# Experts in two groups of tiles, the back stage and most of the combine inside the tile loops

## What is computed

```
h  = layernorm(x) * gamma + beta;  u, z = split(h @ in_proj)      # 256 channels each
uc = silu(conv4(u) + b);  dt, B, C = split(uc @ x_proj)
delta = softplus(dt @ dt_proj + b)
state[t] = exp(delta * A) * state[t-1] + delta * B * uc           # 256 x 16 states, over 2048 steps
y  = (sum_n state * C + uc * D) * silu(z)
x1 = layernorm(2 * x + y @ out_proj)
scores = softmax(x1 @ Wg + bg);  take the 2 best of 8 experts per token
e(x) = gelu(x @ W1[e] + b1[e]) @ W2[e] + b2[e]                    # 128 -> 512 -> 128
out = layernorm(x1 + p1 * e1(x1) + p2 * e2(x1))
```

## Time and profile before

| what | value |
|---|---|
| runs, median of three | 786.08 us (785.85 to 788.13) |
| the profiled execution, its own time | 791.61 us |
| its span, first to last instruction | 789.9 us |
| mean granted clock of TensorE | 0.913 of full |
| busy share: PE, DVE, ACT, POOL | 75%, 85%, 54%, 71% |
| scans, VectorE L1382 | 256, 312.9 us |
| products with C, GpSimd L553 | 128, 301.0 us |
| tiles, VectorE L1533 | 71 |
| scatters, GpSimd L673 | 71, 69.8 us |
| mean DMA rate | 149 GB/s |

### The profile page before, as it was taken

One profiled execution on the slowest core, in us unless ns is written; L12 is line 12 of the kernel. 1 busy time (PEld: TensorE's weight loads), 2 busy tenths in 40 slices (PEclk: granted clock), 3 DMA queues, 4 the chain that ended last, 5 costly groups with the idle time before them and its releaser, 6 DMA issues. The chain is left out here.

```text
span 789.9 us, 11864 instructions
## 1 busy us (share of the span) xinstructions
PE 592.4 (75%) x3055; PEld 290.2 (37%) x3071; DVE 670.4 (85%) x1349; ACT 428.5 (54%) x886; POOL 562.2 (71%) x538
## 2 busy tenths in 40 slices
PE   9768788887887888788788674676440999998920
PEld 4322222222322222222222121211130899998910
DVE  4287999999999999999998999999823688887855
ACT  3858586577467476657746554334110565555515
POOL 3345877776899799889879788878865356665634
PEclk9899999999999999999999788878755999999975
DMA  3095476566579568647556654864003677776644
GB/s 93 17 224 133 101 172 154 120 160 161 133 163 258 130 160 191 141 119 186 136 132 152 144 124 104 200 158 109 28 28 102 169 201 215 209 211 176 194 167 169
DMA packets 51169, 117.34 MB, mean 149 GB/s; under 512 B 8816, under 2 KB 25008, under 8 KB 43040
## 3 DMA queue, kind: packets, MB, share of 16 engines
q1 hardware_dynamic: 45344, 107.20, 55.7%
q0 software_dynamic: 4320, 8.99, 3.5%
q10 hardware_dynamic: 1440, 0.40, 0.2%
HBM read 100.21 MB, written 16.35 MB: 148 GB/s over the span
## 5 line engine op out<-in xcount | busy, mean ns | idle before, releaser
L553 POOL TENSOR_TENSOR hc<-hs,Crep 128x1024 f32<-128x1024 f32 x128 | 301.0, 2357 | 96.1 <-DVE hs L1382 85.8
L1382 DVE TENSOR_TENSOR_SCAN hs<-bank,state,flow 128x512 f32<-128x512 f32 x256 | 312.9, 1267 | 17.8 <-ACT bank L1125 11.6
L1125 ACT ACTIVATE bank<-bank,negA 128x512 f32<-128x512 f32 x256 | 164.1, 659 | 186.2 <-PE bank L798 182.6
L798 PE MATMUL bank<-delta,sel 64*128 64x512 f32 x512 | 156.7, 691 | 96.6 <-DVE hs L1382 96.2
L1365 DVE TENSOR_TENSOR flow<-flow,bank 128x2048 f32<-128x2048 f32 x63 | 142.9, 2268 | 0.0
L1266 ACT ACTIVATE flow<-bank,b1T 128x128 f32<-128x128 f32 x284 | 80.8, 369 | 57.1 <-PE bank L988 28.7
L798 PEld LDWEIGHTS bank<-delta,sel 64*128 64x128 f32 x512 | 41.8, 198 | 188.7 <-DVE hs L1382 163.6
L673 POOL DMA_INDIRECT results<-flow,idn x71 | 69.8, 983 | 33.1 <-issue 31.3
L807 PE MATMUL bank<-hc,kc 128*32 128x512 f32 x512 | 73.2, 647 | 7.8 <-POOL hc L553 7.8
L996 PE MATMUL bank<-w_sb,flow 128*128 x568 | 75.5, 276 | 4.5 <-ACT flow L1266 3.3
L988 PE MATMUL bank<-flow 128*128 128x128 f32 x568 | 76.8, 279 | 0.0
(11 more groups left out here) (196 smaller groups left out, 793.3 us busy)
## 6 DMA issues: line engine op xcount, KB each, us to landing
flow<-du_d SPq DMA_DIRECT2D x63, 1024.0 KB
flow<-L_ffn_W SPq DMA_DIRECT2D x71, 256.0 KB
xg<-xs SPq DMA_DIRECT2D x71, 66.0 KB
du_d<-du SPq DMA_DIRECT2D x28, 128.0 KB
xin<-L_attn_x SPq DMA_DIRECT2D x8, 256.0 KB, 3.6
hs<-results SPq DMA_DIRECT2D x8, 256.0 KB, 4.7
out<-hc SPq DMA_DIRECT2D x8, 256.0 KB, 2.0
results<-flow,idn POOLq DMA_INDIRECT x71
```

The source lines that it names most:

```text
L553: nc.gpsimd.tensor_tensor(hc[:, Q % 2, two, :], hs[:, Q % 2, two, :], Crep[u % 3][:].unsqueeze(1).broadcast_to([P, 2, T]), ALU.mult).then_ ...
L798: ins = nc.tensor.matmul(dbank[2 * odd + i][:], sel[rows, odd, q % 4, :], delta[u % 2][rows, q // 4, :])
L1125: nc.scalar.activation(dbank[G % 4][:], dbank[G % 4][:], ACT.Exp, scale=negA[:, ch:ch + 1]).then_inc(s_ex, 1)
L1382: nc.vector.tensor_tensor_scan(hs[:, Q % 2, j, :], dbank[G % 4][:], flow[Q % 3][:, j, :], state[:, Q // QUADS % 2, Q % QUADS, j:j + 1], AL ...
```

## The change

The constants first: the units are parted into a group of six and one of two, each with its own tiles and its own half of xs.

```diff
-MAXT = 2 * NTOK // P + E - 1
+GROUP_UNITS = (6, 2)
+GROUP_TILES = [2 * T * n // P + E - 1 for n in GROUP_UNITS]
+GROUP_AT = (0, GROUP_TILES[0])
+FACTS = 4
+MAXT = sum(GROUP_TILES)
+SUMS_AT = 62
+GROUP_ROWS = (E * REGION + E) * P
+PLANNED = (14, 29)
```

That makes 55 and 23 tiles, MAXT = 78. The plan is now a function plan(p, step). Its fifteen steps for group 0 (the fourteen of before, and a copy that sets run to the second group's bases) stand behind the scans of the last host, one behind each of g = 8 to 22:

```diff
+                    if 8 <= g < 23 and j == UNITS - 1:
+                        plan(0, g - 8)
```

The tile loop of group 0 starts when these and the rows of units 0 to 5 are there. The buffers of the loop move from flow to rooms that are free by then (pre, relu, hT, gated), and the banks to ones that the back stage doesn't use, so that one bank is left for the transposed tile:

```diff
-                after(pe, e_xe, n - 1)
-                nc.tensor.transpose(xT_bank[n % 2][:, 0:P], xg[:, n % 8, 0:D], ident[:]).then_inc(e_xT, 1)
+                after(pe, e_xe, n)
+                nc.tensor.transpose(xT_bank[:, 0:P], xg[:, n % 8, 0:D], ident[:]).then_inc(e_xT, 1)
```

The back stages of units 6 and 7 go into the loop's iterations: on TensorE at the end of an iteration, on VectorE behind finish_tile, on ScalarE ahead of the gelu, on GpSimd ahead of the scatter. In this order the four pieces:

```diff
+            def back_of_last(n):
+                if n == 0:
+                    add_states(QUADS * UNITS - 2)
+                if n == 2:
+                    add_states(QUADS * UNITS - 1)
+                if n == 3:
+                    ranks(last - 1)
+                if n == 5:
+                    out_proj(last, (0, 1))
+                if n == 6:
+                    out_proj(last, (2, 3))
+                if n == 14:
+                    xn_T(last)
+                if n == 16:
+                    logits(last)
+                if n == 19:
+                    ranks(last)
...
+            def back_of_last(n):
+                if n == 4:
+                    post(last, 1)
+                if n == 5:
+                    dve.wait_ge(s_plan, PLANNED[0] + 1)
+                    ranks(last - 1)
+                if n == 7:
+                    place(last - 1)
+                if n == 8:
+                    residual(last)
+                if n == 9:
+                    back_stats(last)
+                if n == 17:
+                    best_two(last)
+                if n == 18:
+                    one_hots(last)
+                if n == 20:
+                    ranks(last)
+                if n == 23:
+                    place(last)
+                if 24 <= n < 38:
+                    plan(1, n - 24)
...
+            def back_of_last(n):
+                if n == 13:
+                    xns(last)
+                if n == 15:
+                    xnT_evac(last)
+                if n == 20:
+                    gate_exp(last)
+                if 27 <= n < 27 + E:
+                    fill_tail(n - 27)
...
+            for n in range(MAXT + 3):
+                if n == 5:
+                    mask_ranks(last - 1)
+                if n == 9:
+                    places(last - 1)
+                    tag_rows(last - 1)
+                if 10 <= n < 10 + 4 * TT and n % 2 == 0:
+                    list_rows(last - 1, (n - 10) // 2)
+                if n == 11:
+                    back_rstd(last)
+                if n == 19:
+                    shift_ex(last)
+                if n == 22:
+                    mask_ranks(last)
+                if n == 25:
+                    places(last)
+                    tag_rows(last)
+                if 26 <= n < 26 + 4 * TT and n % 2 == 0:
+                    list_rows(last, (n - 26) // 2)
+                if n >= 3:
+                    scatter(n - 3)
+                if SUMS_AT + 3 <= n < SUMS_AT + 3 + 2 * GROUP_UNITS[0] and (n - SUMS_AT) % 2 == 1:
+                    final_rstd((n - SUMS_AT - 3) // 2)
```

The tags are read for four tiles at once, in five instructions on four columns, behind the copy of every fourth tile:

```diff
+            def row_facts(m):
+                n, last = FACTS * m, min(FACTS * m + FACTS, MAXT)
+                ring, those = slice(n % 8, n % 8 + last - n), slice(n, last)
+                rows = xg[:, ring, :]
+                for k in range(n, last):
+                    dve.wait_ge(e_g[k % 8], 16 * (k // 8 + 1))
+                nc.vector.tensor_tensor(is_second[:, ring], rows[:, :, D + 1], expert[:, those], ALU.not_equal).then_inc(e_k, 1)
+                nc.vector.tensor_tensor(is_first[:, ring], rows[:, :, D + 1], expert[:, those], ALU.is_equal).then_inc(e_k1, 1)
+                dve.wait_ge(e_k, m + 1)
+                nc.vector.tensor_tensor(extra[:, ring], is_second[:, ring], rows[:, :, D + 3], ALU.mult).then_inc(e_ex, 1)
+                for k in range(n, last):
+                    after(dve, e_sc[k % 8], 16 * (k // 8))
+                nc.vector.scalar_tensor_tensor(idn[:, ring], is_second[:, ring], float(NTOK), rows[:, :, D],
+                                               ALU.mult, ALU.add).then_inc(e_id, 1)
+                dve.wait_ge(e_ex, m + 1)
+                nc.vector.tensor_tensor(prob[:, ring], extra[:, ring], rows[:, :, D + 2], ALU.add).then_inc(e_pr, 1)
```

```diff
+                if SUMS_AT + 1 <= n < SUMS_AT + 1 + 2 * GROUP_UNITS[0] and (n - SUMS_AT) % 2 == 1:
+                    add_pair((n - SUMS_AT - 1) // 2)
+                    moments2((n - SUMS_AT - 1) // 2)
```

More of the change, by code:

```diff
@@ L468, in _, with rows_ready @@
                 load_w1(n)
[L469 to L479, removed]
+            def rows_ready(p):
+                sp.wait_ge(s_plan, PLANNED[p])
+                sp.wait_ge(s_fill, 32)
+                sp.wait_ge(s_tail, 16 * E * (p + 1))
+                for b in range(B):
+                    sp.wait_ge(s_scat[b], 128 * sum(GROUP_UNITS[:p + 1]) // 2)
+            rows_ready(0)
             def load_sum(u):
@@ L602, in host @@
                 for slot in range(2 * QUADS):
+                    if slot == 15 and not late:
+                        shift_ex(j - 1)
                     times_c(QUADS * j + slot // 2, slot % 2)
@@ L1011, in _ @@
                     output(n - 2, chosen[n - 2])
+                back_of_last(n)
         @block.scalar
@@ L1268, in gelu, with finals @@
                 ins.then_inc(e_ge, 1)
-            act.wait_ge(s_plan, 14)
-            for n in range(MAXT):
-                gelu(n, index(etab[0:1, n:n + 1], mybir.EngineType.Activation, E - 1))
-            for u in range(UNITS):
+            def finals(u):
                 act.wait_ge(s_fr2, 2 * u + 2)
@@ L1279, in _ @@
                 ins.then_inc(s_fin, 1)
+            act.wait_ge(s_plan, PLANNED[0])
+            act.wait_ge(s_dl, 2 * UNITS)
+            for n in range(MAXT):
+                if n == GROUP_AT[1]:
+                    act.wait_ge(s_plan, PLANNED[1])
+                back_of_last(n)
+                if SUMS_AT + 4 <= n < SUMS_AT + 4 + 2 * GROUP_UNITS[0] and (n - SUMS_AT) % 2 == 0:
+                    finals((n - SUMS_AT - 4) // 2)
+                gelu(n, index(etab[0:1, n:n + 1], mybir.EngineType.Activation, E - 1))
+            for u in range(GROUP_UNITS[0], UNITS):
+                finals(u)
         @block.vector
@@ L1493, in _ @@
                 host(j)
-            last = UNITS - 1
-            ranks(last - 1)
-            place(last - 1)
-            post(last, 1)
-            residual(last)
-            back_stats(last)
-            best_two(last)
-            one_hots(last)
-            ranks(last)
-            place(last)
-            drained(dve, fill_of(last, "ranks"))
-            planned = [0]
-            def plan(ins):
-                planned[0] += 1
-                ins.then_inc(s_plan, 1)
-                dve.wait_ge(s_plan, planned[0])
-            plan(nc.vector.tensor_copy(tail[:], run[:]))
-            plan(nc.vector.tensor_tensor(count[:], run[:], base, ALU.subtract))
-            plan(nc.vector.tensor_tensor(over, count[:].unsqueeze(2).broadcast_to([P, E, ROOM]),
-                                         thresholds.unsqueeze(1).broadcast_to([P, E, ROOM]), ALU.is_gt))
-            plan(nc.vector.reduce_sum(tiles[:], over, AX_X))
-            plan(nc.vector.tensor_tensor_scan(cum[:], one8, tiles[:], 0.0, ALU.mult, ALU.add))
-            cums = cum[:].unsqueeze(1).broadcast_to([P, MAXT, E])
-            plan(nc.vector.tensor_tensor(past, numbers.unsqueeze(2).broadcast_to([P, MAXT, E]), cums, ALU.is_ge))
-            plan(nc.vector.tensor_tensor(pastc, past, cums, ALU.mult))
-            plan(nc.vector.reduce_sum(region[:], past, AX_X))
-            plan(nc.vector.reduce_max(first[:], pastc, AX_X))
-            plan(nc.vector.tensor_tensor(within[:], numbers, first[:], ALU.subtract))
-            plan(nc.vector.scalar_tensor_tensor(lrow[:], region[:], float(REGION), within[:], ALU.mult, ALU.add))
-            plan(nc.vector.tensor_scalar(expert[:], region[:], float(E - 1), None, ALU.min))
-            plan(nc.vector.tensor_copy(rtab[:], lrow[:]))
-            plan(nc.vector.tensor_copy(etab[:], expert[:]))
             def x_evac(n):
```

210 lines of the change are left out of this document (124 added, 86 removed).

## The result

The changed kernel takes 817.1 us (median of four runs, 816.4 to 817.7) where the kernel before takes 786.5 (785.9 to 788.1): a ratio of 1.039, 95% interval [1.037, 1.040]. The forecast was slower, 790.5. The direction is right and the size is not: the kernel takes 26.6 us more than forecast. Its profiled execution has a span of 814.9.

A forecast was written before the change was run, and what follows sets the result against it. It took VectorE to bound the hosts, nothing the idle stretch, and TensorE, with VectorE nearly as tight, the tile loop. Terms, including +13.3 for seven more tiles, sum to +4.4 on the median 786.08: 790.5 us, range 779 to 801.

The forecast's parts named there:

- The step that failed: Tile loop: GpSimd takes in its former idle-stretch work over 36 tiles, the ring of eight lending the rest; +0.5 us, bound 8.
- the one on GpSimd as the loop's bound (801): Slower rival, tile loop: a scatter costs GpSimd 1.90 us, not 1.38, adding 10.5 us; 801 us, chance 0.04.
- Back stage off the path: Before the tile loop: group 1 starts once unit 5's rows are listed, first transposition at 574.5 instead of 611.61; −37.1 us.
- plan in the last host: Fifteen VectorE plan steps between scans: 5.8 us of their own plus 3.5 for waits on GpSimd products; +9.3 us.
- the prediction's sign of being wrong (within 6): End of the scans: the prediction is wrong if the last scan ends within 6 us of 569.9.
- The full exclusion (803.5): Slower rival, last host: every two-input plan step waits for a GpSimd product, 16.5 us instead of 3.5; 803.5 us, chance 0.03.
- Insertions in group 1: Group 1's tile loop: added work costs +9.0 us on TensorE, +5.9 on VectorE, +1.6 on ScalarE, +0.5 on GpSimd.
- Tags: VectorE's tile loop: tags for four tiles at once delay the finish in one iteration of four; +2.1 us, bounds 0 and 6.
- Combine in the loop: Group 2's tiles: six units' combine, each alone between finish and copy every second iteration; +13.0 us, half-clock bound 3.2 more.
- Combine out of the end: Kernel's end: six units' combine at 2.20 us each leave it; −13.2 us.
- the rival in which the change cancels: Last host: the plan steps' 3.5 us of waits on neighbours don't occur; 787.0 us, chance 0.20.
- The faster rival: VectorE's tile loop: the freed tag time is usable, so insertions and tags cost less; 781.1 us, chance 0.25.

The follow-up runs named there:

- three edited forms on chip 4: Kernel after with lists writing 512 bytes per row, tags one tile at a time, or each list behind its iteration's scatter: 790.1, 788.9 and 788.5 us.
- doubled scatter: Kernel before with a second scatter at each of 19 tiles: 789.3 us on chip 14, 831.1 us (1.051) on chip 6.
- unchanged kernel: Kernel after with no further edit, against the kernel before: 817.2 us (chip 13), 818.5 (chip 6), 788.4 (chip 7).
- the last experiment: Kernel after with lists behind scatters and VectorE's inserted steps ahead of the finish, on chip 7: 779.9 us, 0.992 of the kernel before.
- lists last alone: Kernel after with each list issued behind its iteration's scatter instead of ahead, on chip 13: 820.1 us, 1.039 of the kernel before.
- four edits: Kernel after without the sixteen lists, with 512-byte list rows, with tags per single tile, or with lists behind scatters: 793.0, 790.1, 788.9, 788.5 us.
- two of the controls: Kernel before with a plain SP DMA, or a GpSimd product, added at 19 tiles, on chip 14: 787.7 and 817.2 us.

## Why the prediction was off, point by point

**The step that failed** is the one on GpSimd: "+0.5, bound 8". It asked whether GpSimd has the time for sixteen lists beside the scatters. It has: on chip 7, and in three edited forms on chip 4, the lists are in the loop and the kernel takes 788.4 to 790.1, within about 2 us of the forecast. What the step did not ask is what close indirect DMAs do to others. In the first measurement, as on 13 and 6, they hold TensorE's completions back: 117.3, 116.5 and 118.1 us for group 1, where chip 7 needs 95.1 (581.25 to 676.38). So this term is 21 to 23 us, and about 5 more between tiles 41 and 64 (50.3 against 44.9 on chip 7), 4 of them in the three tiles at the run of close scatters from tile 49 on. No rival had it: the one on GpSimd as the loop's bound (801) had the right engine and the wrong mechanism, as in the first trace GpSimd never had more than one finished tile waiting for its scatter. Its whole price is 26 us: 818.5 against 792.6 without the lists, on chip 6; or the difference of the ratios, 1.036 and 1.003, of 788.

By the Trainium skill (SBUF — State Buffer, section "Who interferes with whom") DMA contends with no compute engine and TensorE waits for nobody. The three chips without the stall agree: in none of their traces does a gelu of the tile loop start more than 0.41 us behind its product's end. Chips 13 and 6 and the first measurement do not, at 2.1 us for each doubled scatter, and the measurement decides. Whether TensorE's work or only its completions are late, no record shows.

**The rest, against the unchanged kernel on chip 7** (profiled span 789.1, against the forecast's 789.9 + 4.4).
*Back stage off the path and plan in the last host*, −37.1 + 9.3: the first transposition moves from 611.61 to 581.25, −30.4 for −27.8. The plan was 9.3 in the sum and delays the list by 7.0 in the first trace. There its fifteen steps take 9.0 us of VectorE, near the forecast, but the last host, from its first scan to its last, grows by 7.7 only (62.0 to 69.7): oh and taken, which met products before as well, take 3.6 instead of 4.1 in all, and some steps overlap their neighbours. The last scan ends at 576.5, 6.6 us behind 569.9, so the prediction's sign of being wrong (within 6) stayed off by little; it would be 7.7 but for 1.1 us that the hosts before it, unchanged, took less in this trace. Nor are the long steps where the two averages of the earlier trace rows pointed. Four wide or late ones are long, and so is taken; groups by line, VectorE, 520 to 576 us of the kernel after:

```profile
L1502 DVE TENSOR_TENSOR taken<-oh 128x32 bf16<-128x32 f32 x1 | 2.3, 2284 | 0.0
L1547 DVE TENSOR_TENSOR delta<-du,cum 128x440 f32<-128x440 f32 x1 | 1.6, 1570 | 0.0
L1537 DVE TENSOR_TENSOR rest<-count,kc 128x256 f32<-128x256 f32 x1 | 1.5, 1530 | 0.0
L1553 DVE TENSOR_TENSOR within<-kc,first 128x55 f32<-128x55 f32 x1 | 1.4, 1395 | 0.0
L1564 DVE COPY run<-kc 128x8 f32<-128x8 f32 x1 | 1.3, 1267 | 0.0
L1544 DVE TENSOR_TENSOR du<-kc,cum 128x440 f32<-128x440 f32 x1 | 0.6, 591 | 0.0
```

The four long plan steps (L1547, L1537, L1553, L1564) end 0.02 to 0.5 us behind the end of a GpSimd product that they overlap. In the second plan, in the tile loop where GpSimd makes no products, the same lines take 0.42 (L1537, the same shape) and 0.18 (L1553, 23 columns for 55). So a few meet a product for part of it, and most meet none: of the seven steps that the prediction counted as two-input ones three are long. The full exclusion (803.5) did not happen; a copy of eight columns took 1.27, so it is not only two-input steps that are caught.
*Insertions in group 1*, 9.0 + 5.9 + 1.6 + 0.5 and half the tags, 18.1: group 1's 95.1 less 41 times 1.90 is 17.2. Right as a sum; the parts were not separated.
*Tags*: tiles 41 to 64, with nothing inserted, take 44.9 for 43.7 at 1.90: 1.2 for 23 tiles, 4 for 78, above the 2.1, within its bounds.
*Combine in the loop*, +13.0: tiles 64 to 76 take 39.9 against 22.8, +17.1. The 3.2 that the prediction kept as a bound for the half clock has come in on chip 7: the granted clock is 0.91 from 721 to 761. Over these twelve tiles the unchanged kernel takes 39.9 and 40.0 at 0.91 (chips 7 and 6), and 37.7 and 38.3 at 0.95 and 0.96 (first measurement and chip 13). The chip 7 timeline has products of eight matmuls in 2.05 and 1.76 us behind a gap, for 1.06 else:

```profile
731.08 0.29 DVE L1614 COPY hT<-bank 128x128 f32<-128x128 f32 x1
...
731.51 0.31 PE L1028 MATMUL bank<-ident,xg 128*128 128x128 f32 x1 [2.08 <-DVE hT L1614]
...
731.77 2.05 PE L1035 MATMUL bank<-hT,pre 128*128 128x128 f32 x8
...
733.61 1.76 PE L1043 MATMUL bank<-w_sb,relu 128*128 x8
```

In the first trace, at 0.95, the same twelve tiles take 37.7, +14.9.
*Combine out of the end*, −13.2: from the last finish to the end 19.3 in place of 33.3, −14.0.
*A hidden base*: the kernel before does not run at 1.90 throughout. Its 71 transpositions take 137.8 us, 4.8 more than 70 times 1.90, 2.6 of them in the nine tiles at the place shown above. The sum took new tiles from the steady rate and left this in the old ones, which the change did not keep. That is where +4.4 in the sum and about −0.8 in the spans part: the misses of the items above (−2.6, −0.9, +0.6 in tiles 41 to 64, +4.1, −0.8) add up to +0.4, and the base takes 4.8 off.

So without the stall the forecast of 790.5 stands within 2.1 us of the measured 788.4 (+4.4 forecast, +2.1 measured there), and with it it is 27 too low. That closeness is in part luck: the combine's excess and the base's took each other off, and the +2.1 is nearer to the +0.9 of the rival in which the change cancels, though most of the plan's delay, whose absence that rival supposed, did occur. In the first measurement the forecast direction, slower, came true by a cost that the sum did not hold. The faster rival (the hole in VectorE's iteration usable) is refuted for the kernel as changed, and the last experiment shows what it was worth: with the insertions put into that hole, 4 to 8 us.

## The version that is faster

Lists last and insertions ahead of the finish: 779.9, 6 us or 0.8% below the kernel before, on the chip without the stall; 813.0, 22 to 23 above it, on the two with it. The lists' place alone gained nothing on chip 13 (820.1 against 817.2), so the gain is VectorE's. Against lists last alone, on chip 13, it is 7.1, within the 6 to 9 expected there. Against the unchanged kernel I had expected 4 to 7 us; it is 4.2 and 5.5 on the stalling chips and 8.5 on chip 7. On chip 7 the combine's twelve tiles take 32.2 us instead of 39.9, and the granted clock is 1.00 from 715 to 747, with TensorE busy 24.4 of the 32 us. The traces of this kernel on chips 13 and 6 show the same (31.8 and 32.0 at 1.00), so the gain is made here, and part of it is the clock's; on those two chips tiles 41 to 64 take 3 us more than in the unchanged kernel and give some of it back. One such place on chip 7:

```profile
726.40 1.06 PE L1035 MATMUL bank<-hT,pre 128*128 128x128 f32 x8
...
727.29 1.06 PE L1043 MATMUL bank<-w_sb,relu 128*128 x8
727.33 0.16 DVE L1690 TENSOR_SCALAR fnmean<-fmv 128x4 f32<-128x4 f32 x1
727.40 0.28 DVE L1636 TENSOR_TENSOR hT<-bank,b_rep 128x128 f32<-128x128 f32 x1
```

The combine's last step begins 0.04 us behind the start of the next tile's output product, and the finish 0.07 behind that: its steps fill the time in which VectorE waited before. No version was found that is faster than the kernel before on a chip with the stall. To get rid of it the lists would have to leave group 1, and with them the two groups; whether spreading them further apart would do was not tried.

## What to carry to other kernels

Work moved under a full loop has two prices: the time of the engine that does it, and what it does to the others; for close runs of GpSimd's indirect DMAs the first was estimated at 0.5 us and the second was 26 on some chips and nothing on others. Before a cost is read from a pair of rows, look at what every other engine does in that microsecond: the stall stood once in the trace of before, in the very rows used. Run the unchanged kernel in every group of experiments: four edits "cured" it before the cure was seen to be the chip, and two of the controls had been run where there was nothing to control. And insertions into an engine's loop belong where that engine waits in each iteration, which was worth 4 to 8 us here for moving three calls.

## What the runs showed of the hardware

- On chips 13 and 6 and in the first measurement (whose chip is not known, so it may be one of them) three or more indirect DMAs of GpSimd, 1.3 to 1.7 us apart, delay what waits for TensorE by 1 to 5 us, until 0.1 to 1 us behind the end of the last one; in a few places a finish is 1 us late behind only two of them (at 736.2 in the unchanged kernel's trace on chip 13). The steady spacing of 1.9 in the kernel before does not. On chips 14, 4 and 7 long series 1.3 to 1.4 us apart delay nothing. What differs between the chips no run shows, and with one or two chips of each kind by number it may also be a condition that lasts on a chip for some time. The kernel before stands at 789.7 and 790.9 on chips 13 and 6, 785.5, 787.1 and 786.3 on the others; but in the first measurement it stood at 786.5 beside the stalling 817.1, so its own time doesn't tell the kind.
- A GpSimd product of 1.27 us holds a VectorE scaling with one input and a column of scalars, all in SBUF, that had begun 0.6 us earlier, until its own end: 1.95 us for 0.29 at the place shown, and 31.7 us for nineteen. The Trainium skill (SBUF — State Buffer, section "Who interferes with whom") names this kind of instruction among those that can take the port pair shared with GpSimd for their whole length, and says that the first to issue gets it; here the later one got through first, by the records.
- A plain DMA of 64 KB beside each of 19 tiles costs 2.2 us in all on chip 14, less than what one run can tell. On a stalling chip it was not run.
